# Turning attention probabilities on VectorE in 32x32 blocks, and values as products of 32 rows

## The reference

```python
def _L0_attn_ref(x, Wq, Wk, Wv, Wr):          # x: layer-normed input of 4 x 512 x 128
    q = (x @ Wq).reshape(b, s, HEADS, HEAD_DIM)   # 16 heads of 64
    k = (x @ Wk).reshape(b, s, HEADS, HEAD_DIM)
    v = (x @ Wv).reshape(b, s, HEADS, HEAD_DIM)
    scores = SCALE * jnp.einsum('bqhd,bkhd->bhqk', q, k)
    causal = jnp.triu(jnp.ones((s, s), dtype=x.dtype), k=1)
    scores = scores + MASK_PENALTY * causal       # -50 above the diagonal, not -inf
    attn = jax.nn.softmax(scores, axis=-1)
    out = jnp.einsum('bhqk,bkhd->bqhd', attn, v).reshape(b, s, HEADS * HEAD_DIM)
    return out @ Wr
```

## Time and profile before

| | us |
|---|---|
| median of 3 runs | 2090.15 |
| lowest, highest | 2088.08, 2103.39 |
| profiled execution | 2105.09 |
| its span | 2103.2 |
| the dense part in it | up to about 515 |
| TensorE, VectorE, GpSimd, ScalarE busy over the span | 1951.9, 1513.3, 1385.5, 1219.7 |

### The profile page before, as it was taken

The page is one execution under the profiler, slowest core; times in us unless marked ns, Lnnn a source line. Parts: engine busy times, 40 slices in busy tenths (PEclk is TensorE's granted clock), DMA queues, the critical chain, the costliest instruction groups (busy, mean ns, idle before and its releaser), DMA issues.

```text
span 2103.2 us, 71774 instructions
## 1 busy us (share of the span) xinstructions
PE 1951.9 (93%) x28614; PEld 1375.2 (65%) x28614; DVE 1513.3 (72%) x3441; ACT 1219.7 (58%) x2533; POOL 1385.5 (66%) x1360
## 2 busy tenths in 40 slices
PE   8999999998589899998999988999999999999987
PEld 5555555554466677776777666777767776767665
DVE  5666666665577777877877776877878787878763
ACT  5666666664245556665655565556666466666453
POOL 3333443434777878777877868787778777878751
PEclk9999999999799999999999999999999999999998
DMA  4000000000455565455755556555755656545550
GB/s 126 6 4 8 1 6 6 6 1 22 111 120 123 140 149 123 111 131 128 166 118 130 123 125 140 132 121 129 159 124 113 141 121 162 136 105 123 129 125 23
DMA packets 249455, 208.54 MB, mean 99 GB/s; under 512 B 72096, under 2 KB 239780, under 8 KB 248996
## 3 DMA queue, kind: packets, MB, share of 16 engines
q1 hardware_dynamic: 249124, 203.96, 41.8%
HBM read 84.19 MB, written 3.67 MB: 42 GB/s over the span
## 4 chain that ended last, share of the span: by engine, by line
PE 53%; SPq 8%; issue 6%; ACT 3%; POOL 2%; DMA 2%; DVE 1%; ACTq 0%; DVEq 0%; POOLq 0%
PE bank L1147 14%; PE bank L941 12%; PE bank L1126 7%; PE bank L1064 6%; PE bank L1295 5%; PE bank L974 5%; SPq L1012 3%; PE bank L1319 2%; POOL T L1019 2%; DMA RB<-norms 2%; SPq L1036 1%; PE bank L1183 1%; SPq L1005 1%; ACT bank L1047 1%; ACT SQ L947 1%
## 5 line engine op out<-in xcount | busy, mean ns | idle before, releaser
L947 ACT ACTIVATE SQ<-bank 128x512 f32<-128x512 f32 x380 | 227.3, 598 | 461.1 <-PE bank L974 297.7
L1019 POOL TENSOR_TENSOR T<-T,RB 128x512 f32<-128x512 f32 x304 | 377.8, 1276 | 138.0 <-DMA RB<-norms 137.8
L965 POOL TENSOR_TENSOR T<-T 128x512 f32<-128x512 f32 x304 | 386.3, 1275 | 78.8 <-DVE T L960 78.5
L941 PE MATMUL bank<-XT,WQK 128*128 128x256 f32 x1520 | 400.2, 397 | 31.5 <-DVE T L960 22.5
L1147 PE MATMUL bank<-WU,YS 128*128 128x128 f32 x3072 | 380.0, 284 | 11.9 <-issue 8.5
L1147 PEld LDWEIGHTS bank<-WU,YS 128*128 128x128 f32 x3072 | 366.0, 198 | 32.2 <-issue 26.5
L941 PEld LDWEIGHTS bank<-XT,WQK 128*128 128x128 f32 x1520 | 276.5, 194 | 153.0 <-issue 91.3
L682 POOL TENSOR_SCALAR PR<-PR,RI 128x512 f32<-128x512 f32 x256 | 173.7, 693 | 301.0 <-DVE RI L571 299.7
L490 ACT ACTIVATE PR<-PR,NM 128x512 f32<-128x512 f32 x256 | 183.5, 717 | 166.0 <-DVE NM L566 164.9
L959 DVE TENSOR_TENSOR T<-bank,TAB 128x512 f32<-128x512 f32 x304 | 207.9, 684 | 83.8 <-POOL T L965 44.4
L960 DVE TENSOR_TENSOR T<-bank,TAB 128x512 f32<-128x512 f32 x380 | 258.0, 679 | 0.0
(11 more groups left out here) (146 smaller groups left out, 3050.8 us busy)
## 6 DMA issues: line engine op xcount, KB each, us to landing
RB<-norms SPq DMA_DIRECT2D x384, 128.0 KB
QP<-T SPq DMA_DIRECT2D x304, 128.0 KB
KZ<-T SPq DMA_DIRECT2D x304, 128.0 KB, 3.3
TAB<-rotary_dram SPq DMA_DIRECT2D x24, 512.0 KB, 4.4
KZ<-T1F SPq DMA_DIRECT2D x80, 128.0 KB, 3.3
QP<-T1F SPq DMA_DIRECT2D x80, 128.0 KB
WQK<-wqk_halves_dram SPq DMA_DIRECT2D x12, 512.0 KB, 4.2
norms<-RN SPq DMA_DIRECT2D x380, 4.0 KB
```

Source lines behind the costliest of these rows:

```text
L941: m = pe.matmul(b[:, ab * HALF:(ab + 1) * HALF], WQK[n % 3][:, i, ab, :], XT[s % 2][:, hf * HALF:(hf + 1) * HALF], start=True, stop=True)
L947: act.activation(SQ[i][:, :, :], bank[5 * (i % 2)][:, :].rearrange('p (a c) -> p a c', a=2), ACT.Square).then_inc(l_squared.sem, 1)
L965: pool.tensor_tensor(t1, t1, T2[i % 2][:, ::-1, :], ALU.add).then_inc(l_rotated.sem, 1)
L1019: pool.tensor_tensor(t1, t1, RB[:, i:i + 1, :].to_broadcast([P, 2, HALF]), ALU.mult).then_inc(l_scaled.sem, 1)
```

## The change

All of it is in the dense part.

- Probabilities are turned by VectorE, 32x32 blocks in place (`dve_turn`). In a block of 32 partitions the result holds, for queries of 32 rows, the keys of that block: so the four partition groups r hold the same 512 keys for different queries (group r has queries 32r to 32r+31 of each step). PTS gets a new layout for it. TensorE's transposes and both copies go.
- `pe_values` multiplies 32 keys at a time: 16 key blocks x 4 partition groups x 2 heads = 128 products of 32 rows, 64 columns of V and 128 queries, into banks 4 to 7 (one for each group).
- For that V has to lie in each of the four partition groups, with all 512 keys: it is stored to DRAM (`sp_store_v`) and read back four times (`sp_spread_v`) into VR. V itself goes from three buffers to two.
- The copy of the keys moves from VectorE to ScalarE. Queries, keys, V and the output projection use banks 4, 5, 6 and 7.
- The queues are in new order, a loop over units k. On SP later loads are moved behind the first units' V.

```diff
+            VR = [sbl(f'VR{i}', [P, SEQ // WIN, P]) for i in range(2)]
+            vd = [nc.dram_tensor(f'vd{i}', (SEQ, P), F32).ap() for i in range(2)]
-            PTS = [[sbl(f'PTS{i}{e}', [P, TPB, SEQ]) for e in range(2)] for i in range(2)]
+            PTS = [[sbl(f'PTS{i}{e}', [P, SEQ // WIN, TPB, WIN]) for e in range(2)] for i in range(2)]
...
-            def pe_turn(g):
-                for e in range(2):
-                    pe.wait_ge(s_norm, 2 * g + e + 1)
-                    pe.wait_ge(s_pt[e], g)
-                    for k in range(TPB):
-                        i = pe.transpose(bank[4 + e][:, k * P:(k + 1) * P], PR[g % 4][e][:, k * P:(k + 1) * P], ident[:, :])
...
-                    i = pe.matmul(bank[6][e * DH:(e + 1) * DH, :], V[u % 3][:, k, e * DH:(e + 1) * DH], PTS[u % 2][e][:, k, :], start=k == 0, stop=k == TPB - 1)
...
+            def pe_values(u):
+                pe.wait_ge(s_vr[u % 2], 64 * (u // 2 + 1))
+                pe.wait_ge(s_turn, 2 * TPB * (u + 1))
+                pe.wait_ge(s_okept, u)
...
+                for kb in range(SEQ // WIN):
+                    for r in range(4):
+                        rows = slice(r * WIN, (r + 1) * WIN)
+                        for e in range(2):
+                            i = pe.matmul(bank[4 + r][e * DH:(e + 1) * DH, 0:P], VR[u % 2][rows, kb, e * DH:(e + 1) * DH], PTS[u % 2][e][rows, kb, :, :].rearrange('p t q -> p (t q)'), start=kb == 0, stop=kb == SEQ // WIN - 1)
+                i.then_inc(s_av, 1)
...
+            def pe_unit(k):
+                if unit(k):
+                    pe_scores(TPB * k + 0)
...
+                if unit(k):
+                    pe_project_v(k)
...
+                if unit(k):
+                    pe_scores(TPB * k + 1)
+                    pe_scores(TPB * k + 2)
...
+                if unit(k - 1):
+                    pe_values(k - 1)
+                if unit(k):
+                    pe_scores(TPB * k + 3)
...
+                if unit(k + 1):
+                    pe_project_q(k + 1)
+                    pe_project_k(k + 1)
+                if unit(k - 1):
+                    pe_project_out(k - 1)
...
+                o = OT[:, :].rearrange('p (t r q) -> p r t q', t=TPB, r=4)
+                act.activation(o, high[:, :, 0:P].rearrange('p r (t q) -> p r t q', t=TPB), ACT.Copy).then_inc(s_okept, 1)
...
+            def dve_turn(g, e):
                 u, j = divmod(g, TPB)
...
+                dve.wait_ge(s_norm, 2 * g + e + 1)
                 dve.wait_ge(s_av, since(u - 1))
...
+                dve.transpose(PTS[u % 2][e][:, :, j, :], PR[g % 4][e][:, :].rearrange('p (k j) -> p k j', j=WIN)).then_inc(s_turn, 1)
...
+                if unit(k):
+                    dve_mask_max(TPB * k + 0, 0)
+                    dve_mask_max(TPB * k + 0, 1)
+                if unit(k - 1):
+                    dve_turn(TPB * (k - 1) + 3, 0)
...
+                if unit(k - 1):
+                    dve_turn(TPB * (k - 1) + 3, 1)
+                if unit(k):
+                    dve_mask_max(TPB * k + 1, 0)
+                    dve_mask_max(TPB * k + 1, 1)
...
+            def sp_store_v(u):
+                sp.wait_ge(s_vkept, u + 1)
+                sp.wait_ge(s_vr[u % 2], 64 * (u // 2))
+                sp.dma_start(vd[u % 2].rearrange('(t p) d -> p t d', p=P), V[u % 2][:, :, :]).then_inc(s_vd, 16)
+
+            def sp_spread_v(u):
+                sp.wait_ge(s_vd, 16 * (u + 1))
+                sp.wait_ge(s_av, since(u - 1))
+                for r in range(4):
+                    sp.dma_start(VR[u % 2][r * WIN:(r + 1) * WIN, :, :], vd[u % 2].rearrange('(k j) d -> j k d', j=WIN)).then_inc(s_vr[u % 2], 16)
```

More of the change, by code:

```diff
@@ L183, in build @@
             s_turn = event('probs_turned')
-            s_pt = [event(f'probs_kept{e}') for e in range(2)]
+            s_vd = event('v_stored')
+            s_vr = [event(f'v_spread{i}') for i in range(2)]
             s_av = event('values_done')
@@ L213, in build, with turns_before, vos_before @@
             s_vok = event('vo_kept')
+            def turns_before(u):
+                return 1 + len([b for b in range(BATCH - 1) if b * PAIRS + 5 <= u])
+            def vos_before(u):
+                return len([q for q in range(HG) if q * PAIRS + 3 <= u])
             def pe_ln_turn(b):
@@ L228, in pe_project_q @@
                     pe.wait_ge(s_wqkv[0], 16)
[L229 to L233, removed]
+                if p == 0:
+                    pe.wait_ge(s_xnt, b + 1)
+                pe.wait_ge(s_qkept, u)
+                pe.wait_ge(s_okept, since(u - 1))
+                pe.matmul(bank[4][:, :], W0[:, 0, p * P:(p + 1) * P], XNT[:, b * SEQ:(b + 1) * SEQ], start=True, stop=True).then_inc(s_q, 1)
             def pe_project_k(u):
                 b, p = divmod(u, PAIRS)
+                if u == 0:
+                    pe.wait_ge(s_wqkv[1], 16)
                 if p == 0:
                     pe.wait_ge(s_xnt, b + 1)
[L239 to L252, removed]
+                pe.wait_ge(s_kkept, u)
+                pe.wait_ge(s_okept, since(u - 1))
+                pe.matmul(bank[5][:, :], W0[:, 1, p * P:(p + 1) * P], XNT[:, b * SEQ:(b + 1) * SEQ], start=True, stop=True).then_inc(s_kd, 1)
             def pe_project_v(u):
@@ L257, in pe_project_v @@
                     pe.wait_ge(s_wqkv[2], 16)
[L258 to L261, removed]
+                if p == 0:
+                    pe.wait_ge(s_xnt, b + 1)
+                pe.wait_ge(s_vkept, u)
+                pe.wait_ge(s_okept, since(u - 1))
                 for t in range(TPB):
-                    i = pe.matmul(bank[7][:, t * P:(t + 1) * P], XNT[:, b * SEQ + t * P:b * SEQ + (t + 1) * P], W0[:, 2, p * P:(p + 1) * P], start=True, stop=True)
+                    i = pe.matmul(bank[6][:, t * P:(t + 1) * P], XNT[:, b * SEQ + t * P:b * SEQ + (t + 1) * P], W0[:, 2, p * P:(p + 1) * P], start=True, stop=True)
                 i.then_inc(s_v, 1)
@@ L463, in act_ln_keep @@
+                for k in range(-9, UNITS + 12):
+                    pe_unit(k)
             def act_ln_keep(b):
@@ L668, in pool_constants @@
+                for k in range(-9, UNITS + 12):
+                    dve_unit(k)
             def pool_constants():
```

440 lines of the change are left out of this document (213 added, 227 removed).

## The result

The changed kernel takes 2121.77 us (median of 4 runs, 2114.52 to 2131.73) against 2094.2 for the kernel before (4 runs, 2088.08 to 2103.39): a ratio of 1.013, 95% interval 1.007 to 1.019. The forecast was 1998 us, the range 1968 to 2058. The profiled execution has a span of 2116.0 us, 12.8 more than before; these are single executions, and since that of before was the longest of its runs, the traces show about half of the 27.6 us between the medians.

The account below looks back on a forecast made before the run. TensorE bounds by plain throughput; 11.29 + 0.20 + 0.42, plus 0.2 norms and folding and 0.3 stalls, makes 12.4 us a unit against 15.35; over 32 units, less 2, 92 us: 2090 to 1998 us, range 1968 to 2058.

Parts of the forecast that it names:

- The bound, the removed work, the base: Dense part: TensorE bounds by plain throughput; removing transposes takes 3.75 us from a plain unit of 15.04, leaving 11.29.
- The pace of the small products: Values on TensorE: 256 small matmuls limited by columns or issue at about 11.5 ns each, taking 3.6 to 4.0 us.
- rival C: Values: the eight tiles do not work side by side, only two column halves; unit 23.3 us, time 2348; chance 0.05.
- Values as a term of the sum: Values group in each unit: 4.0 us in place of 3.58, so +0.42 us; ends 3.58 and 6.9.
- Rival A: Values: the small products are slow, 5.9 to 6.9 us a unit, time 2058 to 2088 us; chance 0.13.
- over 5 is A: Sign on TensorE's timeline: a values group over 5 us, against the forecast's 4.0, means the small products are slow.
- V by way of DRAM: SP's queue: V stored and read back four times takes 10.3 us, hidden under a cover of 13.6, costing nothing.
- TensorE keeps its clock: Dense part: TensorE stays near full, so its granted clock stays at 1.00, the upper level of 2.4 GHz.
- VectorE, ScalarE, start and end: Per unit VectorE 11.6 us, nearly full, ScalarE 8.0, not bounding; first scores unchanged, start and end +2 us in all.
- rival B: Dense part: VectorE or the chain through it bounds; unit 13.5 us, gain 57, time 2033 us; chance 0.08.

Follow-up runs that it names:

- wide values: Changed kernel with the values as 16 matmuls of 512 moving columns again, summing over the wrong keys: 1987.65 us, ratio 0.948 to the kernel before.
- No spread: Changed kernel with V stored and spread only for the first two units, later units using that old V: 2072.72 us, ratio 0.9875 to the kernel before.

## Why the prediction was wrong, step by step

*The bound, the removed work, the base.* Right. With wide values a unit takes 11.91 us, where the steps (11.29 + 0.20, values at 3.58, norms and stalls 0.5) give 11.5 to 12.0; and the plain unit of the changed kernel from 251.47 to 264.59 is 13.12 us, less its gap of 1.01 12.1, against 12.2 by the sum without norms and foldings.

*The pace of the small products.* Right inside a block: 16 ns a matmul, 256 in 4.1 us; I took 4.0. So the 6.9 us below do not come from a floor under each matmul's start. The eight tiles work side by side, which rules out the mechanism of rival C.

*Values as a term of the sum.* Here the prediction failed: 4.0 us taken, 6.9 measured, 2.9 x 32 = 93 us, the whole forecast gain. I asked how fast the array takes small matmuls, not how fast the queue gets them. The kernel before could have told: on its page one group of small matmuls in the six layers has 48.4 us of idle time ended by issue, and on its timeline such a gap stands directly behind the groups of the earlier trace rows:

```profile
L974 PE MATMUL bank<-SQ,IND 128*32 128x64 f32 x6080 | 118.7, 225 | 48.8 <-issue 48.4
...
705.68 1.10 PE L974 MATMUL bank<-SQ,IND 128*32 128x64 f32 x64
708.06 3.84 PE L1147 MATMUL bank<-WU,YS 128*128 128x128 f32 x32 [1.28 <-issue]
```

The gap at 708.06 lies at place 194 of 256, as in the changed kernel, and ends 1.39 us after the end of a packet of instructions. I had the matmuls ahead of it in my argument as 200 in 3.8 us (by the rows 196, 19.4 ns each), but ended the count just before the gap, priced it as an even rate of 4.9 us, and let a row of four column tiles with just 64 matmuls overrule it. A group of 64 fits in one block and shows nothing of supply; 256 matmuls are two whole blocks. Rival A's dearer end, 5.9 to 6.9 us from a wrong cause (time in proportion to columns), has the measured size by luck: my own sign, "over 5 is A", would have named it, and only the run with half of the columns rules it out. Its 2058 to 2088 us (2090 by its own terms) would still have been too low.

*V by way of DRAM.* Hidden as to its own arrival, as I said: no wait for it in the changed kernel. The 2.3 us that I took for what landing takes besides stand on no row; here the whole store landed in 2.3 us at the median, and a read in 4.9. But I costed a transfer only by whether it is on time. Its second price was delay to another transfer: the long gaps. "No spread" gains 529.86 - 491.36 = 38.5 us in the dense part; 22.3 of it is gaps before the values (78.8 - 56.5) and 5.0 gaps before the output projection (6.3 - 1.3). The other 11.2 us I put down mostly to the clock.

*TensorE keeps its clock.* Wrong. The stretch from the first scores behind the values to the next values takes 251.47 - 241.12 = 10.35 us after the gap of 4.94 and 264.59 - 256.67 = 7.92 after that of 1.01: 2.4 us for one long gap. Six of them would make 14 us, an estimate on the high side, since the stretch at the lower level is half as long behind two of the six; 11.2 are to be explained.

*The sum once more.* A mean unit, (500.88 - 26.50) / 30 = 15.81 us between starts of values: 12.1 base, 0.2 for norms and foldings, 78.8 / 32 = 2.5 gaps in the values, 0.4 in other places, 0.5 for the clock; 0.1 is not accounted for.

*VectorE, ScalarE, start and end.* A turning takes 691 ns long, 0.61 to the next start, as taken; VectorE is busy 372 of 529 us, and with wide values 286 of 300: it is the next bound, as rival B had it, and hardly costs. At the end the six layers' first statistics wait 4.75 us for issue where they waited 1.81, and 4.74 to 4.78 in each other kernel of the new order: 3 us that I had not in the sum.

*What stays open.* That a block waits for its packet is shown, and so is that the packet starts later while V's are under way. Why it does is not: the trace has no time at which the packet was asked for. In three of the six long gaps V's packets ran out within 1 us of its start, as at 237.25; in the other three they ran on beside it. What the 1.1 us ahead of an undisturbed packet and the 1.3 us behind it consist of no run here shows. Nor is it settled why the clock is so much lower with half the columns even without long gaps: the runs show only that less work a matmul goes with it.

## What to carry to other kernels

When a change trades few large matmuls for many small ones, count instructions: here no more than 256, loads and matmuls together, came in 3.45 to 4.0 us, so 512 small ones at a stretch cost 6.9 us and not the 4.1 that the array needs for them. Such gaps read "issue", lie at every 128th matmul, and end some 1.4 us after a packet of the queue "instruction"; a page of the kernel before may have them already. Tiny products that wait for nothing show them best. Start large transfers behind the small products, not in them: that took the change from 1.3% slower to 0.7% faster. Large products put between the small ones halved the gaps but gained no time here, since V and the turnings then came late. And watch the row of the clock behind every gap of several us, or behind two short ones.

## What the runs showed of the hardware

- TensorE gets its instructions in blocks of 16.4 KB or 256 instructions. Undisturbed, a block started 3.45 to 4.0 us after the one before, whether it held 128 matmuls of 128 or of 64 columns; beside transfers of 1.3 MB a unit it took up to 7.3 us. Without the spread the 3.73 us at the median are 1.45 until the next packet starts, 0.95 for the packet and 1.33 until TensorE goes on. The Trainium skill (Runtime: NRT & Kernel Launch, Instruction fetch mechanics) describes that instructions are refilled in blocks of 16 KiB, 256 of them. The trace agrees with the size. The page calls the crossing of a block's boundary mostly hidden, since instructions are dispatched more slowly than blocks are filled; for small tiled products the trace disagrees, with 42 gaps and 78.8 us.
- In the changed kernel the first gap in a unit's values comes after 95 to 229 matmuls, 190 to 458 instructions, depending on where in a block they start. Boundaries inside the values were crossed without a gap where the packet had landed 3 to 8 us before; the packet for the block behind it starts about as a block is entered (0.1 us before it at the soonest) or later, so that no more than one block had arrived ahead. The same section gives TensorE's buffer room for 2048 instructions; no run here shows so many ready.
- After an idle stretch of 4.8 us the granted clock was 0.52 for the next 6.4 us; after one of 1.0 us it was not lowered: the first scores behind it take 1.05 us to the next group. Two short gaps can lower it as well: without the spread, 1.77 and 1.65 us of idle time, 3.7 us apart, were followed by a clock of 0.50 from 180.7 to 184.1 us.
- Less work for each matmul came with a slower kernel: half of the columns, 2106.94 (one run) against 2072.72 us without the spread, at a clock of 0.87 against 0.98; with the spread, 2143.27 against 2121.77 us, at 0.84 against 0.95.
